# A ternary feed-forward layer: rounding the activations on GpSimd, making and rounding the input rows on ScalarE

## What is computed

```python
def _L2_ffn_ref(x, w1, w2):
    EPS = 1e-05
    def _bitlinear(x, w):
        rms = jax.lax.rsqrt(jnp.maximum(jnp.mean(w * w), EPS))
        w_quant = jnp.clip(jnp.round(w * rms), -1.0, 1.0) / rms
        w_quant = jax.lax.stop_gradient(w_quant - w) + w
        scale = 127.0 / jnp.maximum(jnp.max(jnp.abs(x), axis=-1, keepdims=True), EPS)
        x_quant = jnp.clip(jnp.round(x * scale), -128.0, 127.0) / scale
        x_quant = jax.lax.stop_gradient(x_quant - x) + x
        return jnp.einsum('bsd,fd->bsf', x_quant, w_quant)
    h = _bitlinear(x, w1)                       # 256 -> 1024
    h = jax.nn.gelu(h, approximate=False)
    return _bitlinear(h, w2)                    # 1024 -> 256
...
x = x + _L2_xattn_ref(_layernorm(x, axis=-1), ctx_2048, ctx_2048, ...)
x = x + _L2_ffn_ref(_layernorm(x, axis=-1), L2_ffn_w1, L2_ffn_w2)
```

## Time and profile before

| | us |
|---|---|
| median of 3 runs | 1506.44 (1503.74 to 1507.62) |
| the profiled execution | 1507.24 |
| its span, first to last instruction | 1505.5 |

### The profile page before, as it was taken

The page is one execution under the profiler, slowest core; times in us unless marked ns, Lnnn a source line. Parts: engine busy times, 40 slices in busy tenths (PEclk is TensorE's granted clock), DMA queues, the critical chain, the costliest instruction groups (busy, mean ns, idle before and its releaser), DMA issues. The chain is left out here.

```text
span 1505.5 us, 22183 instructions
## 1 busy us (share of the span) xinstructions
PE 1434.2 (95%) x6910; PEld 1030.9 (68%) x6910; DVE 891.9 (59%) x1934; ACT 768.4 (51%) x2122; POOL 528.4 (35%) x519
## 2 busy tenths in 40 slices
PE   4999999899989999999999999999997999999998
PEld 1678777788875556557878888876764666665656
DVE  7898988898985342323454545455677555553322
ACT  4888888899983211110234444444457655553210
POOL 2667577877762000000434242422110333331000
PEclk9999999999999999999999999999999999999999
DMA  5211000200005511112100000000232000011120
GB/s 203 72 52 61 8 5 2 96 2 1 2 1 221 217 51 50 55 49 91 68 1 1 1 1 1 15 15 1 107 144 102 1 1 1 1 29 42 47 68 18
DMA packets 21303, 71.65 MB, mean 48 GB/s; under 512 B 3858, under 2 KB 6290, under 8 KB 18244
## 3 DMA queue, kind: packets, MB, share of 16 engines
q1 hardware_dynamic: 12980, 57.37, 10.3%
q10 hardware_dynamic: 8208, 12.87, 2.7%
HBM read 69.01 MB, written 1.22 MB: 47 GB/s over the span
## 5 line engine op out<-in xcount | busy, mean ns | idle before, releaser
L1193 ACT ACTIVATE l0f_silu<-bank 128x512 f32<-128x512 f32 x48 | 28.5, 597 | 199.0 <-PE bank L1117 189.8
L1296 DVE TENSOR_TENSOR l0f_product<-l0f_silu,bank 128x512 f32<-128x512 f32 x48 | 32.9, 687 | 124.1 <-ACT l0f_silu L1193 124.0
L831 POOL TENSOR_TENSOR l0a_stepped<-l0a_y,l0a_m 128x512 f32<-128x512 bf16 x64 | 73.8, 1154 | 91.1 <-DVE l0a_m L579 89.3
L859 POOL TENSOR_TENSOR l0a_head_rstd<-l0a_head_var,all_minus_half 128x4 f32<-128x4 f32 x96 | 99.7, 1043 | 7.6 <-DVE l0a_head_var L601 7.6
L771 ACT ACTIVATE l0a_work<-bank,l0a_neg_max 128x128 f32<-128x128 f32 x256 | 90.2, 370 | 1.3 <-DVE l0a_neg_max L614 1.3
L1129 PEld LDWEIGHTS bank<-all_weights_a,l0f_hidden 128*128 128x128 f32 x384 | 72.9, 190 | 25.4 <-issue 17.2
L1725 DVE TENSOR_TENSOR all_weights_a<-bank,all_cols 128x512 f32<-128x512 f32 x64 | 43.9, 689 | 77.6 <-PE bank L1560 46.2
L1129 PE MATMUL bank<-all_weights_a,l0f_hidden 128*128 128x256 f32 x384 | 88.9, 379 | 0.0
L431 PEld LDWEIGHTS bank<-l0a_k_t,l0a_q_t 128*128 128x128 f32 x512 | 63.9, 191 | 36.3 <-ACT l0a_q_t L757 31.3
L2318 PE MATMUL bank<-l3a_f_xn_t,all_weights_b 128*128 128x512 f32 x192 | 86.2, 593 | 0.0
L804 ACT ACTIVATE l0a_work<-l0a_work,l0a_row_inv 128x128 f32<-128x128 f32 x256 | 82.3, 409 | 5.6 <-DVE l0a_row_inv L618 5.3
...
## 6 DMA issues: line engine op xcount, KB each, us to landing
...
all_weights_a<-in_l_w_q SPq DMA_DIRECT2D x2, 2048.0 KB, 14.2
l0f_spread<-l0f_weights ACTq DMA_DIRECT2D x32, 128.0 KB, 2.9
...
```

The source lines that it names most:

```text
L831: done = g.tensor_tensor(stepped[:, 0:n], value, step, ALU.add)
L859: g.tensor_tensor(head_rstd[:, m % 2, :], head_var[:, m % 2, :], res.minus_half[:, 0:HU], ALU.pow)\
```

## The change

- ScalarE makes the normalised rows of all pairs (`normalise_in`: Identity with scale and bias columns; `ACT_PAIRS = TILES // 2` is all four pairs) and their rounding (`scale_in`), in place of VectorE. GpSimd makes the offset that the bias needs, VectorE the negated mean.
- VectorE's `round_in` is parted in two: `step_in` (maximum, step, reciprocal) and `round_in` (the clipping alone, behind a wait for ScalarE's rounding).
- GpSimd makes `scale_act` (times the reciprocal plus the constant, then the clipping into `act_q`), in place of ScalarE and VectorE, and the scales `in_scale` and `act_scale`.
- The orders change: VectorE takes maxima first and the later pairs' input behind them; TensorE's `turn_in(2)` stands between `project_l3_values(6)` and `(7)`, `turn_in(3)` behind `turn_act(2)`; ScalarE's `gelu(1)` stands ahead of `keep_in(1)`, and its steps for the later pairs are spread between the Gelus.
- A one-column Gelu is put ahead of `norm_mix(0)`; the load of its table goes with it. `gelu` waits for `in_scale` from GpSimd, `add_narrow` for `act_scale`. (The diff leaves out the declarations.)

```diff
--- before.py
+++ after.py
...
@@ -3152,13 +3160,14 @@
                     wide(t)
                 if t == 3:
                     project_l3_values(6)
+                    turn_in(2)
                     project_l3_values(7)
-                if t % 2 == 1 and t // 2 + 1 < PAIRS:
-                    turn_in(t // 2 + 1)
                 if t == NEXT_TURN:
                     turn_next()
                 if 3 <= t < TILES + 3:
                     turn_act(t - 3)
+                if t == 5:
+                    turn_in(3)
                 if t >= 4:
                     narrow(t - 4)
                 if t in NEXT_PROJECT:
@@ -3234,7 +3243,7 @@
 
             def gelu(t):
                 act.wait_ge(wide_made, t + 1)
-                act.wait_ge(in_q_ready, t // 2 + 1)
+                act.wait_ge(in_scale_ready, t // 2 + 1)
                 if t >= 4:
                     act.wait_ge(act_q_ready, t - 3)
                 for n in range(2):
@@ -3242,10 +3251,21 @@
                                           scale=in_scale[:, t:t + 1])
                 done.then_inc(gelu_done, 1)
 
-            def scale_act(t):
-                act.wait_ge(act_inv_ready, t + 1)
-                act.activation(act_rows[t % 4], act_rows[t % 4], ACT.Identity, bias=magic[:],
-                               scale=act_inv[:, t:t + 1]).then_inc(act_scaled, 1)
+            def normalise_in(p):
+                act.wait_ge(in_rstd_ready, p + 1)
+                for t in (2 * p, 2 * p + 1):
+                    done = act.activation(in_rows[:, t, :], res.x[:, t, :], ACT.Identity, bias=in_offset[:, t:t + 1],
+                                          scale=in_rstd[:, t:t + 1])
+                done.then_inc(in_normed, 1)
+
+            def scale_in(p):
+                act.wait_ge(in_inv_ready, p + 1)
+                if p >= 1:
+                    act.wait_ge(in_q_ready, p)
+                for t in (2 * p, 2 * p + 1):
+                    done = act.activation(in_round[:, t % 2, :], in_rows[:, t, :], ACT.Identity, bias=magic[:],
+                                          scale=in_inv[:, t:t + 1])
+                done.then_inc(in_rounded, 1)
 
             def keep_act(t):
                 act.wait_ge(act_turned, t + 1)
@@ -3269,30 +3289,40 @@
             keep_gates(3)
             keep_values(2)
             keep_values(3)
+            act.activation(spare[:], res.minus_half[:, 0:1], ACT.Gelu)
             norm_mix(0)
             for p in range(PAIRS):
                 if p + 1 < PAIRS:
                     norm_mix(p + 1)
                 shift(p)
+            normalise_in(0)
+            scale_in(0)
             keep_l3_values(3)
+            normalise_in(1)
             keep_l3_values(4)
+            scale_in(1)
             keep_in(0)
             gelu(0)
+            gelu(1)
             keep_in(1)
-            gelu(1)
+            normalise_in(2)
             keep_l3_values(5)
             for t in range(TILES + 1):
-                if t < TILES:
-                    scale_act(t)
                 if 2 <= t + 2 < TILES:
                     gelu(t + 2)
                 if t == 0:
+                    normalise_in(3)
+                    scale_in(2)
+                if t == 1:
                     keep_l3_values(6)
                     keep_l3_values(7)
+                    keep_in(2)
                 if t >= 1:
                     keep_act(t - 1)
-                if t % 2 == 1 and (t + 3) // 2 < PAIRS:
-                    keep_in((t + 3) // 2)
+                if t == 2:
+                    scale_in(3)
+                if t == 3:
+                    keep_in(3)
             act.wait_ge(next_rows_kept, 1)
             act.wait_ge(squares_cleared, 1)
             act.activation(res.l3_squares[:, :, 0:P], heads(res.l3_q_rows[:, 0, :]), ACT.Square)
@@ -3374,23 +3404,32 @@
                 v.tensor_tensor(xt, xt, out_banks[p % 2][:], ALU.add).then_inc(x_done, 1)
                 token_moments(v, res, res.x, [2 * p, 2 * p + 1])
                 pair = slice(2 * p, 2 * p + 2)
+                if p < ACT_PAIRS:
+                    v.tensor_scalar(in_neg[:, pair], res.moments[:, pair, 0], -1.0, None, ALU.mult)
                 v.tensor_scalar(in_var[:, pair], res.moments[:, pair, 1], T_EPS, None, ALU.add).then_inc(in_var_ready, 1)
 
+            def step_in(p):
+                pair = slice(2 * p, 2 * p + 2)
+                if p < ACT_PAIRS:
+                    v.wait_ge(in_normed, p + 1)
+                else:
+                    v.wait_ge(in_rstd_ready, p + 1)
+                    row_pair(in_rows, in_rstd, p)
+                    v.drain()
+                v.tensor_reduce(in_max[:, pair], in_rows[:, pair, :], X, ALU.max, apply_absolute_value=True)
+                v.drain()
+                v.tensor_scalar(in_step[:, pair], in_max[:, pair], T_EPS, 1.0 / 127.0, ALU.max, ALU.mult)
+                v.drain()
+                v.reciprocal(in_inv[:, pair], in_step[:, pair]).then_inc(in_inv_ready, 1)
+
             def round_in(p):
-                pair, tiles = slice(2 * p, 2 * p + 2), (2 * p, 2 * p + 1)
-                v.wait_ge(in_rstd_ready, p + 1)
-                row_pair(in_rows, in_rstd, p)
-                v.drain()
-                v.tensor_reduce(in_max[:, pair], in_rows[:, pair, :], X, ALU.max, apply_absolute_value=True)
-                v.drain()
-                v.tensor_scalar(in_step[:, pair], in_max[:, pair], T_EPS, 1.0 / 127.0, ALU.max, ALU.mult)
-                v.drain()
-                v.reciprocal(in_inv[:, pair], in_step[:, pair])
-                v.tensor_scalar(in_scale[:, pair], in_step[:, pair], ternary.rms[:, 0:1], None, ALU.mult)
-                v.drain()
-                for t in tiles:
-                    v.tensor_scalar(in_round[:, t % 2, :], in_rows[:, t, :], in_inv[:, t:t + 1], ROUND_INT, ALU.mult, ALU.add)
-                v.drain()
+                if p < ACT_PAIRS:
+                    v.wait_ge(in_rounded, p + 1)
+                else:
+                    v.drain()
+                    for t in (2 * p, 2 * p + 1):
+                        v.tensor_scalar(in_round[:, t % 2, :], in_rows[:, t, :], in_inv[:, t:t + 1], ROUND_INT, ALU.mult, ALU.add)
+                    v.drain()
                 if p >= 2:
                     v.wait_ge(in_turned, p - 1)
                 v.tensor_scalar(in_q[:, p % 2, :, :], in_round[:], ROUND_INT, 127.0, ALU.subtract, ALU.min).then_inc(in_q_ready, 1)
@@ -3403,17 +3442,10 @@
                 v.tensor_scalar(act_step[:, t:t + 1], act_max[:, t:t + 1], T_EPS, 1.0 / 127.0, ALU.max, ALU.mult)
                 v.drain()
                 v.reciprocal(act_inv[:, t:t + 1], act_step[:, t:t + 1]).then_inc(act_inv_ready, 1)
-                v.tensor_scalar(act_scale[:, t:t + 1], act_step[:, t:t + 1], ternary.rms[:, 1:2], None, ALU.mult)
-
-            def finish_act(t):
-                a = act_rows[t % 4]
-                v.wait_ge(act_scaled, t + 1)
-                if t >= 2:
-                    v.wait_ge(act_turned, t - 1)
-                v.tensor_scalar(act_q[:, t % 2, :], a, ROUND_INT, 127.0, ALU.subtract, ALU.min).then_inc(act_q_ready, 1)
 
             def add_narrow(t):
                 v.wait_ge(narrow_made, t + 1)
+                v.wait_ge(act_scale_ready, t + 1)
                 v.scalar_tensor_tensor(res.x[:, t, :], out_banks[t % 2][:, 0:D], act_scale[:, t:t + 1], res.x[:, t, :],
                                        ALU.mult, ALU.add).then_inc(t_x_done, 1)
 
@@ -3449,18 +3481,24 @@
             add_to_x(0)
             open_gate(2)
             add_to_x(1)
+            step_in(0)
+            open_gate(3)
             round_in(0)
-            open_gate(3)
+            step_in(1)
             add_to_x(2)
             round_in(1)
             add_to_x(3)
             for t in range(TILES + 3):
                 if t < TILES:
                     scale_of_act(t)
-                if 1 <= t <= TILES:
-                    finish_act(t - 1)
-                if t % 2 == 0 and t // 2 + 2 < PAIRS:
-                    round_in(t // 2 + 2)
+                if t == 1:
+                    step_in(2)
+                if t == 1:
+                    round_in(2)
+                if t == 2:
+                    step_in(3)
+                if t == 3:
+                    round_in(3)
                 if t == NEXT_ROWS:
                     normalise_next()
                 if t == NEXT_XN:
@@ -3492,12 +3530,51 @@
                 g.drain()
                 g.tensor_tensor(offset[:, pair], neg_mean[:, pair], rstd[:, pair], ALU.mult)\
                  .then_inc(rstd_ready, 1)
-            for p in range(PAIRS):
+            def in_rstd_of(p):
                 pair = slice(2 * p, 2 * p + 2)
                 g.wait_ge(in_var_ready, p + 1)
-                g.tensor_tensor(in_rstd[:, pair], in_var[:, pair], res.minus_half[:, pair], ALU.pow).then_inc(in_rstd_ready, 1)
-            g.wait_ge(next_var_ready, 1)
```

(43 more changed lines are left out.)

12 lines of the change are left out of this document (10 added, 2 removed).

## The result

The changed kernel takes 1520.78 us in the median of 4 runs, the kernel before 1506.99 beside it: a ratio of 1.0098 [1.0087, 1.0110], about 14 us or 1% slower. The forecast was 1503.5 with a range from 1500.0 to 1517.0. The profiled execution of the changed kernel took 1523.33 us around a span of 1521.5; it is the slowest of the four, and the other three took 1520.12 to 1521.03.

What follows compares the result with a forecast made beforehand. VectorE was taken to set the pace, ScalarE just behind. The saving, 12.1 - 8T with T = 1.15, came to 2.9 us (1158.5 - 1155.6), so 1506.44 - 2.9 = 1503.5 us, range 1500.0 to 1517.0.

Steps and rivals of the forecast that it cites:

- What bounds the kernel: From 1117 to 1154 us the layer runs at VectorE's pace, ScalarE just behind; GpSimd idles and TensorE has room.
- steps 1 to 3: Stretch's start: in_q at 1116.4, not 1116.9; wide(0) 0.75 us later; first act_inv at 1124.65 instead of 1126.32, 1.7 won.
- the walk: The prediction's seven steps following the changed order on the profiled execution's time axis; sum 2.9 us saved.
- The price T: Time of one 128x1024 tensor_scalar on GpSimd, unknown in the trace; taken as 1.15 us, between 0.95 and 2.08.
- rival A: Slower: at T = 2.08 GpSimd bounds the whole layer; 7.6 us later, plus 2.8 for half clock: 1516.8. Chance 0.14.
- both of the prediction's marks: GpSimd's bound decides from T = 1.5 on; the prediction is wrong if T is above 1.75.
- Steps 4 and 5: Mid-stretch: rounding of input pairs waits for ScalarE; wide(4) at 1133.3, VectorE idle 1133.7 to 1137.4, fifth reciprocal 1140.9.
- Steps 6 and 7: Stretch's end: GpSimd latest from the fifth tile, act_q(7) at 1151.3; 4.33 us more gives 1155.6 against 1158.5.
- priced at +1.15: VectorE's input rounding and GpSimd's passes holding each other off: step 5 would be 1.15 us later, the result 1504.7.
- 11.4 us off VectorE: Work leaving VectorE: 5.7 us over eight tiles and 6.0 over four pairs, less a 0.08 us negation each.
- rival C: More than forecast: T at 0.95, better hand-offs, for instance clock staying at 1.00; 4.5 to 7 us saved, about 1501. Chance 0.22.

Runs made afterwards that it cites:

- e3: The kernel before with only both passes over the activations moved to GpSimd, input rows, scales and orders as before; 1520.55 us, ratio 1.0095.
- e4: The changed kernel with GpSimd's second pass as multiply by 1.0 and add the negated constant, clip to 127 left out; 1506.82 us, ratio 0.9998 to the kernel before.
- e10: The changed kernel, its subtract-and-minimum pass kept, with scale_in(2) and scale_in(3) earlier on ScalarE as in e8; 1522.84 us, ratio 1.0105 to the kernel before.
- e8: e4 with scale_in(2) ahead of normalise_in(3) and scale_in(3) ahead of the fifth Gelu on ScalarE; 1504.62 us, ratio 0.9983 to the kernel before.
- e1: The changed kernel with the clipping of the activations into bf16 back on VectorE; 1506.01 us, ratio 0.9996 to the kernel before.
- e2: The changed kernel with both passes over the activations given back to ScalarE and VectorE; 1509.22 us, ratio 1.0015 to the kernel before.

## Why the prediction was wrong

*What bounds the kernel, and steps 1 to 3:* right, with a drift. On before's axis (0.2 later than the changed kernel's) `wide(0)` went at 1120.66, where before had 1119.40 and the walk 1120.15, and the first reciprocal was ready at 1125.05 (walk 1124.65). The ScalarE form priced from L3215 at 580 ns measured 593 and 596 in the two new lines; the table load went into the wait ahead of `norm_mix(0)` and cost nothing.

*The price T:* the step that failed. The prediction wrote "the unknown price, T, of one 128x1024 `tensor_scalar`" and put the one number into "2T + 0.14 a tile", for two instructions that differ in their operations. For L3555 the halved slope of L831 was right: 1.15 estimated, 1.12 measured. L3559 measured 3.63, also above the "two-input" end of 2.08, which I had called a bound. It wasn't one: L831 shows the price of its own operation with a second input, and what is dear here is the pair of operations, of which the trace of before had no row at all. An operation not in the trace should have kept a price of its own and an open upper end.
With the two prices the working of rival A gives the end of GpSimd's row: 1124.65 + 8 x (1.12 + 3.63 + 0.14) + 1.40 + 1.35 = 1166.5 for the last `act_q`, measured 1167.2 on before's axis; and for the single subtraction, 8 x (1.12 + 2.77 + 0.14), it gives 1159.6, measured 1159.6. So rival A's mechanism, GpSimd the bound of the whole layer, is what happened, where the forecast had it the latest from the fifth tile on only. A's 1516.8 was short by 8 x (4.75 - 4.16) = 4.7 us, for the same wrong price. Its other term, the half clock in the tail, was there in the profiled execution (2.8 estimated, 2.4 measured); in the median it isn't shown, and e3 lost as much without it. The mean of the two passes, 2.37, lies above both of the prediction's marks, 1.5 where GpSimd decides and 1.75 where it is wrong; the marks themselves weren't tested.
The Trainium skill's GPSIMD Engine Reference (section 3.1) gives 1.03 cycles an element for a body of up to two ALU operations, 0.88 us as an estimate; its 1.8 cycles, 1.54 us as an estimate, which the prediction called the usual good case, are there the best case of a tight unrolled loop. The fast pairs (1.04 to 1.39) lie between these two; the other forms, with no more operations, took 2.77 to 4.12, above both, and the measurement decides.

*Steps 4 and 5, the new hand-offs:* shown. VectorE waits 2.00 us for `scale_in(2)` and 3.69 for `scale_in(3)`; in e4, with the price out of the way, 1.99 and 3.50. In the changed kernel they cost nothing (e10), in the fast form they are worth 2 us or so (e8).

*Steps 6 and 7, the sum:* even with T right, 3.4 us (12.1 - 8 x 1.085) would not have come. e4's stretch is 1.9 shorter than before's, what follows it 0.8 longer, its time 1.7 us faster at best by the interval. Of the 1.5 us missing in the stretch 1.3 can be placed: 0.4 were lost ahead of the first reciprocal, 0.3 more up to `round_in(2)` at 1129.7, and 0.6 because that rounding took 1.00 us instead of 0.43 beside GpSimd's pass. That last one is the sentence that I had kept out of the sum: that the two hold each other off, priced at +1.15. The rows show it (1.00 and 1.31 for 0.43, 1.52 for 1.12, 1.22 for 0.40), and by them the rule of the Trainium skill's SBUF - State Buffer (who interferes with whom) agrees for the fast forms. For the slow ones it agrees only in part, as the last section says. Behind the stretch every kernel with both passes on GpSimd took 0.3 to 0.8 us longer than before (the changed one 0.7, e4 0.8), and e1 and e2, without them, 0.1 at most. Why is open: nothing was tried on it.

*The rest:* "11.4 us off VectorE" was about right (its busy time fell by 9.5 us, from 891.9 to 882.4, with some 1.2 us of holding by GpSimd in what is left) and worth nothing while GpSimd was the bound. The clock didn't fall where it had before (1.00 from 1130 to 1141, 0.69 before), as rival C hoped; it fell later instead, while TensorE waited for GpSimd.
